# Graph kernel, first scatter pass: normalised rows kept as three 16-bit parts, products with the stored turned one-hots

## The reference, cut to what matters

```python
gathered = edge_val[:, None] * x[edge_col]        # x is the layer-normalised input
e1 = jax.ops.segment_sum(gathered, edge_row, num_segments=N_NODES)
e2 = e1 * (learnable_diag + 1.0)
e4 = x - e2
out = e4 @ weight + bias
```

## Time and profile before

| | us |
|---|---|
| median of 3 runs | 3029.13 |
| lowest, highest | 3024.15, 3031.56 |
| the profiled execution | 3045.77 |
| its span, first to last instruction | 3044.0 |
| scale_nodes, in the trace | 87.9 to 94.1 |
| scatter pass, first to last indirect DMA | 111.7 to 874.8 |
| message_sums, first matmul | 898.8 |

### The profile page before, as it was taken

One profiled execution on the slowest core, in us unless ns is written; L12 is line 12 of the kernel. 1 busy time (PEld: TensorE's weight loads), 2 busy tenths in 40 slices (PEclk: granted clock), 3 DMA queues, 4 the chain that ended last, 5 costly groups with the idle time before them and its releaser, 6 DMA issues. The chain is left out here.

```text
span 3044.0 us, 41562 instructions
## 1 busy us (share of the span) xinstructions
PE 2111.8 (69%) x12602; PEld 1572.0 (52%) x12602; DVE 1662.4 (55%) x3320; ACT 820.1 (27%) x2162; POOL 1240.6 (41%) x1222
## 2 busy tenths in 40 slices
PE   3365655655639995799623477877777776996995
PEld 1244444444427774699512255555555554335995
DVE  7344444444447778555576476766776767403222
ACT  6222222222200002233214132323332322432331
POOL 0366666666650000355303666555655551001221
PEclk9677776677669998799856788778888878997998
DMA  2344444444348853322321444444444443300113
GB/s 74 105 157 148 154 152 149 152 154 145 133 151 297 292 196 104 121 71 72 101 66 56 135 125 123 115 118 120 131 121 120 119 115 95 116 9 20 39 36 104
DMA packets 192123, 366.16 MB, mean 120 GB/s; under 512 B 47573, under 2 KB 102632, under 8 KB 191525
## 3 DMA queue, kind: packets, MB, share of 16 engines
q1 hardware_dynamic: 135472, 207.05, 21.2%
q0 software_dynamic: 56160, 156.43, 16.7%
q10 hardware_dynamic: 274, 0.00, 0.0%
HBM read 232.23 MB, written 131.07 MB: 119 GB/s over the span
## 5 line engine op out<-in xcount | busy, mean ns | idle before, releaser
L1936 POOL DMA_INDIRECT att_rows<-hdram,top_ix x488 | 503.2, 1031 | 357.7 <-issue 341.4
L756 POOL DMA_INDIRECT mtab<-msgs_rw,msgs_ix x488 | 486.9, 998 | 381.1 <-ACT msgs_rw L718 190.8
L645 PE MATMUL msgs_p_m<-nodes_n,msgs_hott 128*128 x976 | 368.3, 539 | 60.8 <-issue 41.2
L2008 PE MATMUL att_p_acc<-att_msg,att_hot 128*128 128x264 f32 x976 | 309.4, 471 | 54.5 <-DVE att_total L2181 13.6
L578 DVE TENSOR_TENSOR msgs_rw<-msgs_p_m,msgs_sorted 128x1024 f32<-128x1024 f32 x122 | 149.2, 1223 | 350.8 <-PE msgs_p_m L645 132.4
L645 PEld LDWEIGHTS msgs_p_m<-nodes_n,msgs_hott 128*128 128x128 f32 x976 | 252.9, 272 | 130.4 <-issue 84.2
L2038 ACT ACTIVATE att_enc<-att_p_z 128x1024 f32<-128x1024 f32 x122 | 124.9, 1024 | 564.3 <-remote 275.8
L2008 PEld LDWEIGHTS att_p_acc<-att_msg,att_hot 128*128 128x128 f32 x976 | 212.4, 229 | 114.7 <-issue 42.5
L1960 PE MATMUL att_p_h<-heads_parts,att_hz 128*128 x1464 | 218.2, 298 | 54.5 <-issue 37.5
L826 PE MATMUL sums_part<-sums_rows,sums_hot 128*128 128x256 f32 x976 | 224.3, 388 | 32.2 <-DVE sums_hot L801 31.9
L1348 PE MATMUL exp_y<-exp_own,exp_ht 128*128 128x256 f32 x1032 | 239.0, 379 | 2.4 <-issue 2.4
(11 more groups left out here) (376 smaller groups left out, 3581.5 us busy)
## 6 DMA issues: line engine op xcount, KB each, us to landing
sums_rows<-mtab SPq DMA_DIRECT2D x122, 520.0 KB, 4.6
etab<-msgs_et SPq DMA_DIRECT2D x122, 288.0 KB
att_hz<-etab SPq DMA_DIRECT2D x122, 288.0 KB
first_w<-in_L_ffn_w SPq DMA_DIRECT2D x16, 512.0 KB
ffn0x_w<-in_L_ffn_w SPq DMA_DIRECT2D x16, 512.0 KB
ffn_w<-in_L_ffn_Wd SPq DMA_DIRECT2D x8, 1024.0 KB, 10.6
mtab<-msgs_rw,msgs_ix POOLq DMA_INDIRECT x488
att_rows<-hdram,top_ix POOLq DMA_INDIRECT x488
```

The lines of the kernel that those rows point to most:

```text
L645: last = T.matmul(p_m[g % 2][:, q, :], hott[g % 2][:, q, :], node, start=True, stop=True)
L756: nc.gpsimd.indirect_dma_start(mtab, bass.IndirectOffsetOnAxis(ap=ix[:, g, q:q + 1], axis=0), rw[g % RS][:, q, :], None).then_inc(s_free[g ...
L1936: nc.gpsimd.indirect_dma_start(rows[:, g % RS, q, :], None, hdram, bass.IndirectOffsetOnAxis(ap=ix1[:, g, q:q + 1], axis=0)).then_inc(s_ro ...
L2008: last = T.matmul(p_acc[g % 2][:, 0:HW], hot[g % 2][:, q, :], msg[g % 2][:, q, :], start=(q == 0), stop=(q == G - 1))
```

## The change

The normalised rows are split, once, into three 16-bit parts whose sum is the float32 value. The split happens in `scale_nodes`, in five chunks of five tiles: ScalarE copies n to 16 bits (first part), VectorE subtracts it from n (`rest`), ScalarE copies the rest to 16 bits (second part), VectorE subtracts again and writes the third part. VectorE now computes all 25 tiles of n. The parts (25 x 3 x 256 in 16 bits) lie in the place of the first weights of experts 6 to 15, whose ten loads are moved behind the last product of the pass. The products of the scatter pass take the 16-bit turned one-hots from `et` and accumulate three products of 256 columns for each; `hott` and its copy are gone. `scale_nodes` now gives its own buffers back before the pass.

```diff
-    hott = [a.sb(f"hott{s}", [P, G, P]) for s in range(2)]
...
-                if g % 6 == 5 and g // 6 < E0:
+                if g % 6 == 5 and g // 6 < LATE:
...
             small_weights(sp, A, wts, s_wts)
+            sp.wait_ge(s_mm, NG)
+            for e in range(LATE, E0):
+                sp.dma_start(wts["w1"][:, e], A["L0_ffn_w1"][e].rearrange("(k p) f -> p k f", p=P)).then_inc(s_w1, 16)
             store_seg(NB - 1)
...
-                node = n[:, bass.ds(b, 1), :].rearrange("p a c -> p (a c)")
-                pe.wait_ge(s_hott, g + 1)
+                node = nparts[:, bass.ds(b, 1), :, :].rearrange("p a i c -> p (a i) c")
+                pe.wait_ge(s_eth, g + 1)
                 if g >= 2:
                     pe.wait_ge(s_rw, g - 1)
                 for q in range(G):
-                    last = T.matmul(p_m[g % 2][:, q, :], hott[g % 2][:, q, :], node, start=True, stop=True)
+                    turned = et[g % ES][:, (G + q) * P:(G + q + 1) * P]
+                    for i in range(3):
+                        last = T.matmul(p_m[g % 2][:, q, :], turned, node[:, i, :], start=(i == 0), stop=(i == 2))
                 last.then_inc(s_mm, 1)
...
                 act.wait_ge(s_turned, g + 1)
-                if g >= 2:
-                    act.wait_ge(s_mm, g - 1)
-                S.copy(hott[g % 2][:].rearrange("p q d -> p (q d)"), p_hot[g % 2][:, 0:G * P]).then_inc(s_hott, 1)
                 if g >= ES:
+                    act.wait_ge(s_mm, g - ES + 1)
                     act.wait_ge(s_store[g % ES], 16 * (g // ES))
                 S.copy(et[g % ES][:, G * P:ET], p_hot[g % 2][:, 0:(G + 1) * P]).then_inc(s_eth, 1)
...
-            for i in range(0, NT, 2):
-                V.tensor_scalar(n[:, i, :], x[:, i, :], mean[:, i:i + 1], scale[:, i:i + 1], ALU.add, ALU.mult).then_inc(s_n, 1)
+            def rows(c):
+                for i in range(c * TB, c * TB + TB):
+                    last = V.tensor_scalar(n[:, i, :], x[:, i, :], mean[:, i:i + 1], scale[:, i:i + 1], ALU.add, ALU.mult)
+                last.then_inc(s_n, 1)
+            def first(c):
+                dve.wait_ge(s_high, c + 1)
+                if c >= 2:
+                    dve.wait_ge(s_low, c - 1)
+                V.tensor_tensor(rest[c % 2][:], n[:, at[c]], nparts[:, at[c], 0, :], ALU.subtract).then_inc(s_rest, 1)
+            def second(c):
+                dve.wait_ge(s_mid, c + 1)
+                V.tensor_tensor(nparts[:, at[c], 2, :], rest[c % 2][:], nparts[:, at[c], 1, :], ALU.subtract).then_inc(s_low, 1)
+            rows(0)
+            for c in range(full):
+                if c + 1 < full:
+                    rows(c + 1)
+                first(c)
+                if c:
+                    second(c - 1)
+            second(full - 1)
...
+            def high(c):
+                act.wait_ge(s_n, c + 1)
+                S.copy(nparts[:, at[c], 0, :], n[:, at[c]]).then_inc(s_high, 1)
+            def middle(c):
+                act.wait_ge(s_rest, c + 1)
+                S.copy(nparts[:, at[c], 1, :], rest[c % 2][:]).then_inc(s_mid, 1)
```

More of the change, by code:

```diff
@@ L36 @@
 ZROW = NPAD
+LATE = 6
 BIG = 2.0 ** 100
@@ L449, in _, with message_rows @@
                         sp.wait_ge(s_back, 16 * (d + 1))
-def message_rows(nc, a, A, cst, n, tab1, starti, nbucket, gb, dump, mtab, etab, segtab, ix1, penn, wts, s_w1, s_wts):
+def message_rows(nc, a, A, cst, nparts, tab1, starti, nbucket, gb, dump, mtab, etab, segtab, ix1, penn, wts, s_w1, s_wts):
     H8 = H
@@ L473, in message_rows @@
     p_cnt = p_end[:, P:P + BC]
-    (s_chain, s_ix, s_hot, s_turned, s_hott, s_eth, s_mm, s_rw, s_id, s_go, s_fields, s_rcb, s_rct, s_place, s_prep,
+    (s_chain, s_ix, s_hot, s_turned, s_eth, s_mm, s_rw, s_id, s_go, s_fields, s_rcb, s_rct, s_place, s_prep,
      s_line, s_seg, s_back, s_isend, s_cnt, s_penn, s_clear, s_lines) = (a.sem(m) for m in (
-         "chain", "ix", "hot", "turned", "hott", "eth", "mm", "rw", "id", "go", "fields", "rcb", "rct", "place", "prep",
+         "chain", "ix", "hot", "turned", "eth", "mm", "rw", "id", "go", "fields", "rcb", "rct", "place", "prep",
          "line", "seg", "back", "isend", "cnt", "penn", "clear", "lines"))
@@ L837, with scale_nodes @@
 PF = 10
-def scale_nodes(nc, a, x, n, mean, scale):
-    shift, s_shift, s_n = a.sb("shift", [P, NT]), a.sem("shift"), a.sem("n")
+def scale_nodes(nc, a, x, n, nparts, mean, scale):
+    shift, rest = a.sb("shift", [P, NT]), [a.sb(f"rest{s}", [P, TB, C]) for s in range(2)]
+    s_shift, s_n, s_high, s_rest, s_mid, s_low = (a.sem(m) for m in ("shift", "n", "high", "rest", "mid", "low"))
+    full = NT // TB
+    at = [slice(c * TB, c * TB + TB) for c in range(full)]
     with nc.Block() as block:
@@ L849, in _ @@
             V.tensor_tensor(shift[:], mean[:], scale[:], ALU.mult).then_inc(s_shift, 1)
-            for i in range(0, NT, 2):
-                V.tensor_scalar(n[:, i, :], x[:, i, :], mean[:, i:i + 1], scale[:, i:i + 1], ALU.add, ALU.mult).then_inc(s_n, 1)
+            def rows(c):
[18 more added lines that the diff above has]
+            second(full - 1)
         @block.scalar
         def _(act):
-            act.wait_ge(s_shift, 1)
-            for i in range(1, NT, 2):
-                nc.scalar.activation(n[:, i, :], x[:, i, :], ACT.Identity, bias=shift[:, i:i + 1],
-                                     scale=scale[:, i:i + 1]).then_inc(s_n, 1)
-            act.wait_ge(s_n, NT)
+            S = nc.scalar
+            def high(c):
[4 more added lines that the diff above has]
+                S.copy(nparts[:, at[c], 1, :], rest[c % 2][:]).then_inc(s_mid, 1)
+            high(0)
+            for c in range(full):
+                if c + 1 < full:
+                    high(c + 1)
+                middle(c)
 def row_broadcast(sp, to, vec, sem):
@@ L2253, in build @@
                     n = n0.sb("n", [P, NT, C])
-                    scale_nodes(nc, Pool_(nc, cn, "ln0"), x, n, mean, scale)
+                    nparts = wts["w1"][:, LATE:].rearrange("p e k f -> p (e k f)").bitcast(BF16)
+                    nparts = nparts[:, 0:NT * 3 * C].rearrange("p (t i c) -> p t i c", i=3, c=C)
                     with ExitStack() as c2:
-                        message_rows(nc, Pool_(nc, c2, "msgs"), A, cst, n, tab1, starts[1], buckets[1], gb[1], dump, mtab,
+                        scale_nodes(nc, Pool_(nc, c2, "ln0"), x, n, nparts, mean, scale)
+                    with ExitStack() as c2:
+                        message_rows(nc, Pool_(nc, c2, "msgs"), A, cst, nparts, tab1, starts[1], buckets[1], gb[1], dump, mtab,
                                      etab, segtab, ix1, penn, wts, s_w1, s_wts)
```

## The result

The changed kernel is **slower**: 3073.69 us, median of 4 runs (3067.86 to 3085.19), against 3026.64 for the kernel before, 4 runs (3022.43 to 3031.56). The ratio is 1.0147, 95% interval 1.0116 to 1.0178, some 47 us. The forecast was 3042 us, 2995 to 3070: the sign was the likelier one, the size is out of the range. The profiled execution took 3077.43 us, 3.7 above its median, while that of before (3045.77) stood 19.1 above the 3026.64; so the two profiles differ by 31.7 us and not by 47. Five single executions of 3412 us and more, which lie far above the others of their kernel, are left out of every comparison in this document.

A forecast was written before the change was run, and what follows sets the result against it. The scatter pass was taken to run at GpSimd's pace with gaps. Split +16.7, pass -4 and loads 0 sum to +12.7 us on the 3029.13 us median: 3042 us, range 2995 to 3070.

The forecast's parts named there:

- The split: scale_nodes: VectorE scales all 25 rows and does ten subtractions on the path; +16.7 us, bounds +14.4 and +23.7.
- The products' own length: Scatter pass: twelve 16-bit matmuls a group take 1.43 or 2.7 us by clock, saving about 0.8 us a group.
- Rival E: Scatter pass products: still limited by weight loads, no saving, 3046 us; chance within the forecast's 0.50.
- The loads, "0": End of the scatter pass: ten moved weight loads end with 13 us to spare before message_sums' first matmul; 0 us.
- rival D: End of the scatter pass: the ten loads delay the last DMAs and first rows, up to +18, 3060 us; chance 0.09.
- What reaches the path: Scatter pass: shorter products only wait earlier for the same late completion; only gaps outside that pattern shrink, -4 us.
- the bounded extreme of a second gap of 4.4: Scatter pass: the slow bound on the -4 us, a second such gap on the other side of each round.
- The reading of the gaps: Scatter pass: small-matmul bursts hold back TensorE's completions until GpSimd's DMAs run dry; 4.4 us in 30 rounds, 132 us.
- Rival C: Scatter pass: more TensorE instructions get more completions held back, 66 us, 3108 us; a third gives 3064; chance 0.14.
- Rival A: Scatter pass: late completions move with TensorE's work, so shorter product chains save 41 us, 3004 us; chance 0.20.
- Rival B: Scatter pass: float32 products cause the held-back completions, so all 137.5 us of gaps may go, 2908 us; chance 0.07.
- The mark set for C: Scatter pass: GpSimd's two waits rising above 160 us, from about 135, would show more completions held back.

The follow-up runs named there:

- e1: The changed kernel with the old float32 products and widened one-hots back, split and late loads kept; 3064.3 us, 1.0061 of the kernel before.
- f3: The changed kernel with scaling and split inside the pass's block, all ten subtractions on VectorE, late loads behind the sums' row loads; 2699.6 us, 0.9996 of the kernel before.
- series 3: Both kernels unchanged, and each with an added GpSimd pause per round; the kernel before took 2698.1 us, the changed kernel 1.0035 of it.
- f1: The changed kernel with scaling and split inside the pass's block, three last subtractions on GpSimd, late loads behind the sums' row loads; 3061.0 us, 1.0088 of the kernel before.
- e3: The changed kernel with only the high part's product, one in place of three; 3075.8 us, 1.0110 of the kernel before.
- r_after2: The changed kernel, unchanged, compared once more with the kernel before; 3061.9 us, 1.0086.
- series 2: Four edits looking for what lengthens the pass: loads added back, late loads without split, products not accumulated, another operand; ratios 0.9994 to 1.0081 of the kernel before.
- d1_again: The kernel before with GpSimd waiting, each round, for group 1's row DMAs to land before group 2's, run again; 3035.1 us, 0.9976 of the kernel before.
- series 3 and 5: The two sets of runs in which the kernel before took 2698.1 and 2699.9 us, the changed kernel 1.0035 and 1.0036 of it.
- e4: The kernel before with each one-hot transposed twice, as many TensorE instructions a round as the changed kernel; 3044.7 us, 1.0002 of the kernel before.
- e2: The kernel before with three unaccumulated 16-bit products on the rows' upper halves, no widened copy, no split, loads as before; 3033.9 us, 0.9968 of the kernel before.
- d1: The kernel before with GpSimd waiting, each round, for group 1's row DMAs to land before group 2's; 2781.2 us, 1.0302 of the kernel before.

## Why the prediction was wrong

**The split: right.** +16.7 forecast. VectorE's first instruction of the pass stands at 110.67 against 94.59, +16.1; the subtractions take 1.48 us (1.45 forecast). e1's pass of 763.0 shows that the split did not lengthen the pass, and f3 that it need not all lie on the path: 6.7 us of it went beside the pass's set-up.

**The products' own length: right.** 1.51 and 2.74 us a group (1.43 and 2.7 forecast). Rival E falls.

**The loads, "0": wrong by 4.2 us** (2.7 in series 3). What failed here is "ten issues of about 0.45 us, still ahead of GpSimd's last DMA": they took 1.29 us each. It is a small form of rival D, and f1 and f3, with the loads behind the sums' row loads, have the 24 us back.

**What reaches the path, "No product lies in the gap" and -4: this is the step that failed.** It took the place of the held completion as given, the round's fourth group, from one round of the trace, and 4.4 us in each of 30 rounds from it. Already the trace of before has it otherwise: 25 gaps ahead of the fourth group, 3.5 us each, and 8 of 5.0 us ahead of a round's first. It was mostly the third in the profile of the kernel after, the first in e3, mostly the fourth again in r_after2. With it at the third group, one product and the next round's set-up chain do lie in a second gap (398.62 to 401.36 above), and that pass was +19.7 us where -4 was forecast. It was not the bounded extreme of a second gap of 4.4, but a shift from one of 4.4 to two of 3.2 and 1.9.

**How much of the 47 us is the change's** stays partly open. By start and tail, 20 us. The other 27 are the pass and the spread between executions: another profile of the same kernel had a pass of 763.0, and its comparison gave 1.0086, +24 us, against 1.0147. That pass, too, has none of the -4, but +24 us would have lain inside the range: how far out the forecast came hangs on which series is taken. The two intervals do not meet, and single runs of the kernel before go from 3022 to 3054 in such series, so the interval of four runs against four was too narrow for what the change is worth. Why completions were held at the third group in one profile of the kernel after and at the fourth in the other is open. An interaction of the parts, sought in series 2, was not found. Without held completions the change costs 1.0035 and 1.0036 in two series: by the profiles of series 3, +15.9 for the start, +2.7 for the tail and -10.7 for the pass, 8 in all, where the medians differ by 11.

**The reading of the gaps: not borne out.** That completions come free only once GpSimd has run dry is wrong: 16 of the 51 "remote" waits of before end while its DMAs run on. d1_again shows that a pause takes a gap's place, not that it sets completions free. That the burst of small matmuls makes the hold is wrong as a cause that suffices: in series 3 and 5 the same burst holds nothing. Rival C's cause, more instructions, falls by e3 and e4, though its smaller form (3064) was nearest to the result. Rival A's gain is not there either: e3's one product, with the shortest chain, made the pass longer. Rival B, that float32 products cause the holds, falls by e2, whose pass has 139.2 us of gaps above 0.6 us against 140.2. The mark set for C, waits above 160 us, was not reached (148.5); part of the growth was booked as "issue" (gaps above 0.6 us: 161 against 140).

## What to carry to other kernels

When an engine waits for something that comes late for no reason of the program, do not cost an edit by where that wait lies in one round: count over the whole pass how often it lies there, shift the work a little and see whether it stays with its instruction. An engine that stands idle until a completion arrives sees it arrive behind its own last work each time; that is no sign that this work held it back. Measure both kernels in more than one series before a difference of 1% is told as the edit's; here the same pair gave 1.0147, 1.0086, 1.0035 and 1.0036. And where GpSimd issues the transfers, see what VectorE has under way when each begins: here a compare of two SBUF operands made such an instruction up to 0.5 us longer.

## What the runs showed of the hardware

The same program took 2698 and 2700 us in two series and 3027 to 3044 in four others, with no median between. By one profile of each kind it is 124 us less in the scatter pass and 209 in the attention pass, the two passes with 488 indirect DMAs each, and 11 us after the latter; up to the scatter pass and between the two passes the profiles agree within 1 us. What sets the kind isn't known; the runs of one series were all of one kind, and two series that named the same chip number came out one of each. In the kind that takes 3040 us VectorE and ScalarE wait up to 10 us (12.7 in e3) for completions of TensorE that come late, and GpSimd runs into such a wait about once in a round of four groups. In the other kind the profile of the kernel before has none in the pass. A sum of what edits bring holds only within one kind: the pause of d1 is worth -2 us in one and +83 in the other.

An indirect DMA instruction of GpSimd (0.97 us) that begins while VectorE's one-hot compare is under way ends some 0.84 us after the compare, up to 1.50 us in all; one that begins before the compare is not lengthened.
